# Wide attention on one core: projections as column tiles of 64, transposes of the maxima behind the value products, the output's division in four pieces

## The reference

```python
q, k, v = (xn @ w for w in (w_q, w_k, w_v))      # 4 x 1024 x 1024: 16 heads of 64
attn = softmax(q_h @ k_h.T * 64 ** -0.5)         # per batch and head, 1024 x 1024
o_h = attn @ v_h
```

## Time and profile before

| what | value |
|---|---|
| median of 3 runs | 4124.36 us (4118.59 to 4128.01) |
| profiled execution | 4125.23 us, its span 4123.6 us |
| PE busy | 2990.2 us, 73% |
| DVE busy | 2493.7 us, 60% |
| ACT busy | 1764.8 us, 43% |
| POOL busy | 1370.3 us, 33% |
| the stage that is changed | about 46 to 1411 us of the span |

### The profile page before, as it was taken

How to read it: one execution, slowest core, us unless ns; L and a number is a source line. 1 busy time by engine, 2 the same in 40 slices (tenths; PEclk the granted TensorE clock), 3 DMA queues, 4 the chain that set the end, 5 groups by cost and what they waited for, 6 DMA issues and landing times. The chain is left out here.

```text
span 4123.6 us, 63956 instructions
## 1 busy us (share of the span) xinstructions
PE 2990.2 (73%) x20107; PEld 1317.5 (32%) x20108; DVE 2493.7 (60%) x3634; ACT 1764.8 (43%) x2751; POOL 1370.3 (33%) x795
## 2 busy tenths in 40 slices
PE   4999999999999657995425999998971201906984
PEld 1333333333333353332211222222651101604662
DVE  5666666666666237888645899994333746324533
ACT  2555555555545204443105888887430200412332
POOL 1878777878787401000042000000014041060000
PEclk9999999999999878997557999999995555958965
DMA  2111111111111221000151111111112130121012
GB/s 72 31 47 40 47 40 47 40 47 42 45 45 42 98 103 48 1 0 2 79 151 34 26 34 28 31 30 26 46 57 63 46 105 14 43 54 35 10 34 62
DMA packets 247968, 190.15 MB, mean 46 GB/s; under 512 B 146199, under 2 KB 192143, under 8 KB 246152
## 3 DMA queue, kind: packets, MB, share of 16 engines
q1 hardware_dynamic: 236616, 164.09, 14.0%
q0 software_dynamic: 11264, 24.99, 2.1%
HBM read 104.31 MB, written 64.16 MB: 41 GB/s over the span
## 5 line engine op out<-in xcount | busy, mean ns | idle before, releaser
L309 POOL TENSOR_TENSOR attn_esum<-attn_esum,attn_prob 128x1024 f32<-128x1024 f32 x384 | 904.5, 2356 | 126.2 <-ACT attn_prob L460 105.3
L520 DVE TENSOR_REDUCE attn_half_max<-attn_peek 128x2 f32<-128x1024 f32 x512 | 627.0, 1225 | 439.0 <-PE attn_peek L347 439.0
L826 DVE TENSOR_REDUCE attn_half_max<-attn_peek 128x2 f32<-128x1024 f32 x512 | 589.1, 1218 | 146.4 <-PE attn_peek L746 83.4
L460 ACT ACTIVATE attn_prob<-attn_score 128x1024 f32<-128x1024 f32 x512 | 512.3, 1021 | 331.6 <-PE attn_score L330 330.9
L810 ACT ACTIVATE attn_prob<-attn_score 128x512 f32<-128x512 f32 x1024 | 556.0, 596 | 211.7 <-DMA experts_raw<-in_L_ffn_sh_up 138.2
L378 PE MATMUL attn_acc<-attn_prob,attn_v 128*64 128x512 f32 x2048 | 496.2, 605 | 0.1
L1816 POOL DMA_DIRECT2D sorted_y<-experts_y x28 | 21.2, 759 | 1041.5 <-DVE experts_y L1914 1041.5
L776 PE MATMUL attn_acc<-attn_prob,attn_v 128*32 128x256 f32 x4096 | 340.0, 405 | 9.1 <-ACT attn_out L802 7.7
L760 PE MATMUL attn_score<-attn_qe,attn_ke 49*128 49x512 bf16 x1024 | 206.8, 400 | 99.7 <-ACT attn_prob L810 39.2
L746 PE MATMUL attn_peek<-attn_ke,attn_qe 48*128 48x512 bf16 x1024 | 209.1, 405 | 51.1 <-DMA attn_ke<-k 39.1
L347 PE MATMUL attn_peek<-attn_hi 64*128 64x512 f16 x1024 | 200.0, 387 | 44.8 <-DVE attn_half_max L520 44.8
(11 more groups left out here) (449 smaller groups left out, 4693.1 us busy)
## 6 DMA issues: line engine op xcount, KB each, us to landing
attn_xb<-attn_x_all SPq DMA_DIRECT2D x66, 256.0 KB, 2.5
attn_invB<-inv SPq DMA_DIRECT2D x64, 256.0 KB, 4.1
o<-attn_out SPq DMA_DIRECT2D x32, 512.0 KB, 2.7
out_o<-o SPq DMA_DIRECT2D x8, 2048.0 KB
experts_x<-sorted_x SPq DMA_DIRECT2D x112, 64.0 KB, 1.8
sorted_y<-experts_y POOLq DMA_DIRECT2D x28, 256.0 KB, 2.7
attn_qe<-q SPq DMA_DIRECT2D x192, 32.0 KB
attn_ke<-k SPq DMA_DIRECT2D x192, 32.0 KB
```

What stands on the lines that cost most here:

```text
L309: nc.gpsimd.tensor_tensor(own, before, prob[:, u % NPROB, :, :], ALU.add).then_inc(added, 1)
L460: nc.scalar.activation(prob[:, u % NPROB, :, :], score[:, u % 2, :, :], ACT.Exp).then_inc(exped, 1)
L520: V.tensor_reduce(half_max[:, half, :, t], peek[:], AX.X, ALU.max, negate=True).then_inc(maxed, 1)
L826: V.tensor_reduce(half_max[:, half, PAIR * pair:PAIR * (pair + 1), t], peek[:, m % NPEEK, :, :], AX.X, ALU.max, negate=True).then_inc(maxe ...
```

## The change

- `project` issues its products in pairs of column tiles of 64 output partitions: twice as many products, each with half the columns of weights.
- In step 2 `total` moves ahead of the value products and `turn` behind them (it now waits for `sums_read`); in step 6 `turn` moves behind the value products.
- `scores` waits for `shift_ready` only ahead of the product that reads `shift`, not ahead of the tile.
- `invert` moves from step 5 to step 4, behind the second maximum; `normalise` becomes four instructions of 128 by 256: behind the second maximum of step 5, behind `spread` in step 6, between the maxima of step 7, and behind the second of step 7. `store` waits for all four.

```diff
+    PARTS_OUT = 4
+    INVERT_STEP, OUT_PARTS = 4, {(5, 1): 0, (6, 1): 1, (7, 0): 2, (7, 1): 3}
...
-                sp.wait_ge(normed, i + 1)
+                sp.wait_ge(normed, PARTS_OUT * (i + 1))
...
-                if u % UPC == 0:
-                    pe.wait_ge(shift_ready, NC * i + u // UPC + 1)
...
+                    if ks is None and t == 0:
+                        pe.wait_ge(shift_ready, NC * i + c + 1)
...
-                            last = mm(small[:, t * P:(t + 1) * P], xb[px][:, slot, (half * TPC + t) * P:(half * TPC + t + 1) * P],
-                                      w[pw][:, slot, WHICH[what], :], start=(k == 0), stop=(k == 2))
+                            for h in range(heads):
+                                tokens = slice((half * TPC + t) * P + h * HD, (half * TPC + t) * P + (h + 1) * HD)
+                                last = mm(small[rows_of(h), t * P:(t + 1) * P], xb[px][:, slot, tokens], w[pw][:, slot, WHICH[what], :],
+                                          start=(k == 0), stop=(k == 2))
...
-                        last = mm(small[:], w[pw][:, slot, WHICH[what], :], xb[px][:, slot, half * CH:(half + 1) * CH],
-                                  start=(k == 0), stop=(k == 2))
+                        for h in range(heads):
+                            last = mm(small[rows_of(h), :], w[pw][:, slot, WHICH[what], rows_of(h)], xb[px][:, slot, half * CH:(half + 1) * CH],
+                                      start=(k == 0), stop=(k == 2))
...
-                        elif n == 3 and first:
-                            pe.wait_ge(shift_ready, 2)
                         elif n == 3:
-                            pe.wait_ge(sums_read, i)
+                            pe.wait_ge(shift_ready, NC * i + 2)
...
+                    if s == SUM_STEP and not first:
+                        if final:
+                            pe.wait_ge(shift_ready, NC * i + 1)
+                        else:
+                            pe.wait_ge(lo_ready, 4 * (i + 1) + 3)
+                        total(i - 1, 1 - slot)
+                    weigh(i, slot, u, first)
+                    weigh(i, slot, u + 1, first)
+                    if s == Q0_STEP and not final:
+                        pe.wait_ge(lo_ready, 4 * (i + 1) + 2)
+                        project(i + 1, 1 - slot, 2)
                     elif s == TURN1_STEP:
-                        if final:
+                        if not first:
+                            pe.wait_ge(sums_read, i)
+                        elif final:
...
-                    weigh(i, slot, u, first)
-                    weigh(i, slot, u + 1, first)
-                    if s == Q0_STEP and not final:
-                        pe.wait_ge(lo_ready, 4 * (i + 1) + 2)
-                        project(i + 1, 1 - slot, 2)
-                    elif s == SUM_STEP and not first:
-                        pe.wait_ge(shift_ready, NC * i + 2)
-                        total(i - 1, 1 - slot)
...
-            def normalise(i, slot):
-                dve.wait_ge(inv_back, DMA * heads * (i + 1))
-                dve.wait_ge(read_out, NC * (i + 1))
-                V.tensor_tensor(out[:, slot, :, :], out[:, slot, :, :], invB[:], ALU.mult).then_inc(normed, 1)
+            def normalise(i, slot, k):
+                if k == 0:
+                    dve.wait_ge(inv_back, DMA * heads * (i + 1))
+                    dve.wait_ge(read_out, NC * (i + 1))
+                c, q = k * NC // PARTS_OUT, slice(k * CH // NC % CH, (k * CH // NC % CH) + CH // NC)
+                V.tensor_tensor(out[:, slot, c, q], out[:, slot, c, q], invB[:, c, q], ALU.mult).then_inc(normed, 1)
...
-                    elif s == SUM_STEP + 3 and not first:
-                        invert(i - 1)
+                    if (s, 0) in OUT_PARTS and not first:
+                        normalise(i - 1, 1 - slot, OUT_PARTS[s, 0])
                     beside(u + 1)
...
-                    if s == STEPS - 1 and not first:
-                        normalise(i - 1, 1 - slot)
+                    if s == INVERT_STEP and not first:
+                        invert(i - 1)
+                    if (s, 1) in OUT_PARTS and not first:
+                        normalise(i - 1, 1 - slot, OUT_PARTS[s, 1])
```

More of the change, by code:

```diff
@@ L595, in _ @@
             invert(NI - 1)
-            normalise(NI - 1, 1)
+            for k in range(PARTS_OUT):
+                normalise(NI - 1, 1, k)
 def narrow_attention_stage(nc, ident, q_d, k_d, v_d, o_d, l_d, max_d, beside):
```

## The result

The changed kernel took 4143.47 us (median of 8 runs) against 4119.6 us before (8 runs): ratio 1.0058, 95% interval 1.0046 to 1.0070, 24 us slower. Its profiled execution has a span of 4145.9 us (before 4123.6). The forecast was 35 us slower.

A forecast was written before the change was run, and what follows sets the result against it. PE, 95% busy, sets the pace. Gains of 2.26 and costs of 2.82 us make +0.56 an item; with 0.66 for the clock over 30 items, 36.6 us, less small corrections: 4159 us, range 4093 to 4197.

The forecast's parts named there:

- gains: Sum of PE time saved by tilings, the step 6 transpose and the division: 2.26 us an item.
- costs: Sum of new waits and delays an item, before any fall of the granted clock: 2.82 us.
- PE's gains: Projections share the value products' tiling; six tiling switches go at 0.11 each, 0.66 us an item; doubled products cost nothing.
- Transposes: Step 6's wait of 0.35 us for the merge goes; step 2's passes to `total`, gaining nothing; its merge costs 0.10.
- Division: At look B of step 0 PE's wait of 1.25 us for the long division goes.
- Piece 0: First quarter division waits for inverses, then tile 12's addition; ends 7.63 us after step 5's look A, delaying step 6's look B 2.08.
- Step 7: Second quarter division waits for the addition of tile 14, so look B comes 0.60 us late.
- race of piece 2: In step 7 the third quarter division slips in 0.13 us ahead of tile 15's addition; losing: 4199 us, chance 0.09.
- Item without the clock: Net change of an item before any lower clock: 2.82 less 2.26, +0.56 us.
- Clock: Step 6's PE pause of about 1.9 us may drop the clock to 1.2 GHz: bounds 0 and 1.1, taken 0.66 an item.
- Items 0 and 31: First and last items have no division among maxima and only gain, about 1 us each.
- inverses back in time: Rival: inverses arrive before the first quarter division needs them, -0.86 us an item, 4097 us; chance 0.14.

The follow-up runs named there:

- tiles alone: The kernel before with only the projections issued as column tiles of 64: ratio 0.9951, 19 us faster.
- division alone: The kernel before with only the division in four pieces and the reciprocal in step 4: ratio 1.0203, 81 us slower.
- one division: The changed kernel with one division at the end of step 7 and the reciprocal in step 5, as before: ratio 0.9953 to the kernel before.
- few additions: Changed kernel and kernel before, each with POOL's additions of tiles 2 to 7 and 10 to 15 cut to one column of each 512: 0.9854 and 0.9856.
- reciprocal earlier: The changed kernel with the reciprocal in step 3 instead of 4: ratio 0.9922 to the kernel before, 31 us faster.
- late division: Changed kernel with the reciprocal in step 5 and the whole division of item i-2 between the maxima of step 0: ratio 0.9852 to the kernel before.

## Why the prediction was right, and which sizes were not

The distances from look to look of the two kernels can be set side by side, half a step at a time (medians over the items whose clock stays up). The gains are 2.35 us an item (2.26 expected), the costs 2.84 (2.82 expected).

- *PE's gains* (0.66 for the tilings): right in kind, 0.79 measured. The doubled products run side by side. A v projection takes 0.69 to 0.70 instead of 0.77, and the value products behind it, now in the same tiling, 1.82 instead of 1.87. So neither the trace nor the tiles alone show a plain weight load that holds PE up.
- *Transposes* (0.35 in step 6, 0.10 lost in step 2): 0.30 and 0.18. `total` waits longer in step 2 than the transpose did.
- *Division* (1.25 at look B of step 0): 1.26.
- *Piece 0* (end 7.63 after look A of step 5, look B of step 6 later by 2.08): right. It ends at 1037.00 - 1029.38 = 7.62, the look is 2.09 late. But the arrival of the inverses was off. I had taken one row, 6.98 us in item 31; over the 30 items with maxima they come 6.4 to 6.8 us after the reciprocal, in the item shown 6.51. So they miss the start of tile 12 by 0.12 to 0.56 us and not by 0.7. The 2.08 came out right all the same, because the end of piece 0 hangs on tile 12 and not on the inverses. In the division alone the margin was crossed three times.
- *Step 7* (0.60 at look B; race of piece 2 won by 0.13): right. 0.52, and piece 2 lasts 0.41, tile 15 starting at 1043.19, 0.22 behind it. All 30 items with maxima went this way.
- *Item without the clock* (+0.56): measured 41.58 - 41.09 = +0.49.
- *Clock*: the mechanism was right, its size was not. A stretch at 1.2 GHz costs 1.3 us an item (42.9 - 41.6; I had 1.1), but it comes in 9 of 30 items, not in six of ten: 9 x 1.3 = 12 us instead of 20. This is 8 of the 11 us by which the forecast was too high; the item without the clock is 2 more. The share was taken between two other pauses, not from any row. It is not the pause's length that decides in which items the clock falls, for all 30 pauses are alike to 0.02 us. The stretches come in every third or fourth item, with 126.3 or 167.3 us from one start to the next in both executions of the changed kernel, so the moment at which the pause comes seems to matter; what it is measured against stays open. Behind 1.79 + 0.79 us of pauses close together the clock fell in 23 of 26 items.
- *Items 0 and 31*: expected 2 us faster together; the start of the stage gained 2.2, its end none. No weight.
- *The rival "inverses back in time"* was priced at -0.86 an item; with the reciprocal in step 3 it measured -0.95. Its three waits of 0.39, 0.32 and 0.55 measured 0.37, 0.32 and 0.54.

Shown: the loss is the division's (division alone +2.0%, one division -0.5%), and it needs the additions (few additions) and the late inverses (reciprocal earlier) together. Not tried: pieces of other sizes at the same places, and pieces at the late place, so how much of the late division's gain is owed to its place and how much to its being whole is not shown.

## What to carry to other kernels

In this kernel an instruction of DVE with two operands in SBUF, met by one of POOL's additions, costs what is left of that addition, each time anew. Dividing it multiplies these waits, so first look for the gap in POOL's timeline and put the whole thing there. When a step is moved nearer to a transfer that it needs, take the transfer's spread over many items from the trace, not one sample, and compare it with the moment at which another engine takes the port. And when a wait of the fastest engine is removed, check who sets the pace of what stands behind it: here the additions kept their times and took the gain back.

## What the runs showed that was not expected

- Two waits of which neither costs PE much at look B of step 6 (0.24 us for the inverses without additions, nothing for the additions with early inverses) cost 2.09 us together, since the first delivers the instruction just behind the start of the next addition.
- The same pause of 1.92 us is followed by a lower clock in some items and not in others, in the same share in two executions (9 of 30 items in each, in part not the same ones).
- The swap of merge and low part brought 0.51 us an item where 0.35 were expected.
